# AdaLN and mixture-of-experts kernel: conditioning weights selected by predicated copies, one of two transposed halves copied by VectorE

## The reference, cut to what matters

```python
def _L0_cond_ref(x, subjects, weights, bias):
    w = weights[subjects]              # (128, 32, 32), one of 8 tables for each batch
    b = bias[subjects]
    out = jnp.einsum('bct,bcd->bdt', x, w)
    return out + b[:, :, None]

def _L0_ffn_ref(x, gate_w, w1, w2, w3, sw1, sw2, sw3):
    ...
    scores = jax.nn.softmax((xt @ gate_w.T).astype(jnp.float32), axis=-1)   # 8 experts, top 2
    ...
    z = jax.nn.silu(xt @ sw1.T) * (xt @ sw3.T) @ sw2.T                      # shared, 352 wide
    return (y + z).reshape(B, S, D)

x = x + _L0_ffn_ref(_L0_cond_ref(x, itok_B_0_7, L0_cond_weights, fside_8xS_0), ...)
x = x + _L1_ffn_ref(_L1_cond_ref(x, ...), ...)     # low-rank adapters, then an fp8 gated network
```

## Time and profile before

| | |
|---|---|
| median of 3 runs | 429.93 us (429.85 to 430.27) |
| the profiled execution's own time | 429.1 us |
| its span | 427.3 us |
| TensorE busy | 412.4 us, 97% |
| VectorE busy | 309.2 us, 72% |
| ScalarE busy | 249.0 us, 58% |
| GpSimd busy | 193.2 us, 45% |
| granted TensorE clock | full in all 40 slices |

### The profile page before, as it was taken

One profiled execution on the slowest core, in us unless ns is written; L12 is line 12 of the kernel. 1 busy time (PEld: TensorE's weight loads), 2 busy tenths in 40 slices (PEclk: granted clock), 3 DMA queues, 4 the chain that ended last, 5 costly groups with the idle time before them and its releaser, 6 DMA issues.

```text
span 427.3 us, 8683 instructions
## 1 busy us (share of the span) xinstructions
PE 412.4 (97%) x2954; PEld 331.7 (78%) x2954; DVE 309.2 (72%) x728; ACT 249.0 (58%) x552; POOL 193.2 (45%) x198
## 2 busy tenths in 40 slices
PE   7999789999999999999999999999999999999996
PEld 5567578887889999999999998885665756657553
DVE  5987898997987666666666663759587786777845
ACT  2987544667335665556655654438475494664854
POOL 2404229900544544455445403646575575754020
PEclk9999999999999999999999999999999999999999
DMA  8998300000145554655555622321143232322111
GB/s 250 381 388 297 99 0 2 1 2 0 54 128 179 167 161 144 181 160 158 165 159 176 152 87 74 88 74 51 52 134 95 66 111 74 113 87 61 49 51 50
DMA packets 37290, 50.44 MB, mean 118 GB/s; under 512 B 4504, under 2 KB 30496, under 8 KB 37248
## 3 DMA queue, kind: packets, MB, share of 16 engines
q1 hardware_dynamic: 29600, 31.53, 21.8%
q0 software_dynamic: 6512, 17.71, 15.7%
q10 hardware_dynamic: 1136, 0.65, 0.6%
HBM read 32.18 MB, written 17.69 MB: 117 GB/s over the span
## 4 chain that ended last, share of the span: by engine, by line
PE 81%; ACT 8%; DVE 7%; issue 2%; DMA 2%; POOL 0%; DVEq 0%; ACTq 0%; POOLq 0%
PE bank L1132 16%; PE bank L1134 16%; PE bank L1133 15%; PE bank L1408 13%; PE bank L1423 6%; PE bank L1294 4%; ACT xtr L468 2%; PE bank L1333 2%; PE bank L1332 2%; PE bank L1314 2%; PE bank L1374 2%; ACT xtT L482 2%; PE bank L1222 1%; DVE hsf L761 1%; DMA pick<-in_pick 1%
## 5 line engine op out<-in xcount | busy, mean ns | idle before, releaser
L403 POOL DMA_INDIRECT xg<-kept,perm x71 | 68.1, 959 | 91.2 <-PE bank L1294 54.9
L1408 PE MATMUL bank<-h,wg 128*128 128x512 fp8e4 x256 | 61.6, 380 | 0.2 <-ACT ff L642 0.2
L1132 PE MATMUL bank<-w13h,xgl 128*128 x142 | 48.9, 344 | 0.4 <-issue 0.4
L1408 PEld LDWEIGHTS bank<-h,wg 128*128 128x128 fp8e4 x256 | 22.2, 98 | 33.9 <-ACT ff L642 13.3
L410 POOL DMA_INDIRECT ga<-slots_out,slot x32 | 32.8, 1026 | 33.3 <-SPq L349 17.3
L963 DVE TENSOR_TENSOR hrl<-bank,hrh 128x256 fp32r<-128x256 f32 (+1 forms) x36 | 15.1, 421 | 44.2 <-issue 36.5
L1134 PE MATMUL bank<-w13h,xgh 128*128 x142 | 45.5, 320 | 0.0
L1133 PE MATMUL bank<-w13l,xgh 128*128 x142 | 45.5, 320 | 0.0
L640 ACT ACTIVATE gel<-bank 128x512 bf16<-128x512 f32 x64 | 40.2, 627 | 6.4 <-PE bank L1408 3.2
L410 POOL DMA_INDIRECT gb<-slots_out,slot x32 | 37.7, 1178 | 9.8 <-issue 9.8
L642 ACT ACTIVATE ff<-bank 128x512 bf16<-128x512 f32 x64 | 40.6, 635 | 0.0
(11 more groups left out here) (199 smaller groups left out, 1167.8 us busy)
## 6 DMA issues: line engine op xcount, KB each, us to landing
slots_out<-yr SPq DMA_DIRECT2D x35, 256.0 KB
xres<-in_x SPq DMA_DIRECT2D x7, 512.0 KB, 10.3
kept<-xtr SPq DMA_DIRECT2D x7, 512.0 KB, 7.4
out_x<-fin SPq DMA_DIRECT2D x7, 512.0 KB
w13raw<-in_rw SPq DMA_DIRECT2D x8, 352.0 KB, 4.3
w2raw<-in_rw SPq DMA_DIRECT2D x8, 256.0 KB, 5.6
wgst<-in_wgate SPq DMA_DIRECT2D x16, 128.0 KB
xg<-kept,perm POOLq DMA_INDIRECT x71
```

The costliest lines, as they stand in the source:

```text
L403: pool.indirect_dma_start(out=xg[:, i % 2, j, :], out_offset=None, in_=kept, in_offset=bass.IndirectOffsetOnAxis(perm[:, 2 * i + j:2 * i + ...
L1132: pe.matmul(dst, al, bh, start=first, stop=False, skip_group_check=True)
L1408: ins = pe.matmul(bank[bk][:, :], wg8[:, kk, half, c * P:(c + 1) * P], h8[:, k, kk, :], start=(kk == 0), stop=(kk == KC - 1))
```

## The change

Four edits, and what follows from them. (1) The table is laid out with the choice ahead of the output channel. `wrow` is cleared once, and `select_rows` makes eight predicated copies for each group, one for each choice: where the mask of choice e is set, the table's row of choice e is copied to `wrow`. Each waits for the one before. `prod` is gone. (2) The masks `hot` lie in PSUM, bank 5, columns 0 to 255. Bank 5 being taken, the bias matmul and both halves' raw logits go to bank 4 (columns 0 to 31; 0 to 127 and 128 to 255), and the transposed logits to bank 5, columns 0 to 127, and bank 4, columns 256 to 383; `router(4)` waits until the first half's raw logits are out. (3) ScalarE's `keep_xT` copies only the first half, and VectorE gets a `keep_xT` for the second, with a semaphore `xtT_half`; whoever waited for `xtT_ready` waits for both. (4) VectorE's queue: selections 0 to 3; for i = 4 to 7 `keep_xT(i-4)`, then selection i; then `keep_xT(4)` to `keep_xT(7)`; then `shared_weight_lo(0)` and all the rest as before.

```diff
-        tabr = at("tabr", [P, CH, E], F32, early)
-        hot = at("hot", [P, TILES, E], F32, early)
+        tabr = at("tabr", [P, E, CH], F32, early)
         wrow = at("wrow", [P, TILES, CH], F32, early)
-        prod = at("prod", [P, GT, CH, E], F32, early)
...
+        hot = bank[5][:, 0:TILES * E].rearrange("p (t e) -> p t e", e=E)
+        logit_psum = [bank[5][:, 0:P], bank[4][:, 2 * P:3 * P]]
...
-            pool.wait_ge(s("xtT_ready"), 2)
+            pool.wait_ge(s("xtT_ready"), 1)
+            pool.wait_ge(s("xtT_half"), 1)
...
             def keep_xT(i):
-                for c in range(KC):
-                    act.wait_ge(s("T_done"), i * KC + c + 1)
-                    act.activation(xT_of(i)[:, c, :], bank[6 + c][:, :], ACT.Copy).then_inc(s("xtT_ready"), 1)
+                act.wait_ge(s("T_done"), i * KC + 1)
+                act.activation(xT_of(i)[:, 0, :], bank[6][:, :], ACT.Copy).then_inc(s("xtT_ready"), 1)

             def keep_raw(h):
                 act.wait_ge(s("raw_done"), h + 1)
-                act.activation(lraw[:, h, :], bank[4 + h][:, 0:P], ACT.Copy).then_inc(s("raw_kept"), 1)
+                act.activation(lraw[:, h, :], bank[4][:, h * P:(h + 1) * P], ACT.Copy).then_inc(s("raw_kept"), 1)
...
+            dve.memset(wrow[:, :, :], 0.0).then_inc(s("hot_ready"), 1)
             dve.wait_ge(s("front_in"), 16)
...
             def select_rows(t0, t1):
-
-                link(dve.tensor_tensor(prod[:, 0:t1 - t0], *picks(t0, t1), ALU.mult))
-                dve.tensor_reduce(wrow[:, t0:t1, :].rearrange("p t j -> p (t j)"),
-                                  prod[:, 0:t1 - t0].rearrange("p t j e -> p (t j) e"), AX.X, ALU.add
-                                  ).then_inc(s("rows_ready"), 1)
+                shape = [P, t1 - t0, CH]
+                for e in range(E):
+                    ins = dve.copy_predicated(wrow[:, t0:t1, :], hot[:, t0:t1, e:e + 1].bitcast(I32).broadcast_to(shape),
+                                              tabr[:, e:e + 1, :].broadcast_to(shape))
+                    if e < E - 1:
+                        link(ins)
+                ins.then_inc(s("rows_ready"), 1)
                 selected[0] += 1
                 dve.wait_ge(s("rows_ready"), selected[0])
...
-            for i in range(1, GROUPS):
+            def keep_xT(i):
+                dve.wait_ge(s("T_done"), i * KC + 2)
+                dve.tensor_copy(xT_of(i)[:, 1, :], bank[7][:, :]).then_inc(s("xtT_half"), 1)
+
+            for i in range(1, 4):
                 select_rows(i * GT, (i + 1) * GT)
+            for i in range(4, GROUPS):
+                keep_xT(i - 4)
+                select_rows(i * GT, (i + 1) * GT)
+            for i in range(4, GROUPS):
+                keep_xT(i)
             shared_weight_lo(0)
...
             def transpose_xt(i):
                 if i >= 1:
-                    pe.wait_ge(s("xtT_ready"), i * 2)
+                    pe.wait_ge(s("xtT_ready"), i)
+                    pe.wait_ge(s("xtT_half"), i)
...
             def router(i):
                 h, m = i // HALF, i % HALF
-                pe.wait_ge(s("xtT_ready"), i * 2 + 2)
+                pe.wait_ge(s("xtT_ready"), i + 1)
+                pe.wait_ge(s("xtT_half"), i + 1)
+                if m == 0 and h:
+                    pe.wait_ge(s("raw_kept"), h)
```

More of the change, by code:

```diff
@@ L264, in adaln_ffn @@
         for name in ("ids_in front_in pick_in table_in const_in shapes_in gate_in sw_in hot_ready rows_ready c_link c_prep out_ready bias_made bias_ready "
-                     "cond_done xt_ready T_done xtT_ready gate_spread raw_done raw_kept logit_psum "
+                     "cond_done xt_ready T_done xtT_ready xtT_half gate_spread raw_done raw_kept logit_psum "
                      "m_sub m_exp r_ob r_rank r_digits r_lanes r_places r_listed r_perm r_expert sw_hi sw_split "
@@ L297, in _ @@
         def _(sp):
-            sp.dma_start(tabr[:, :, :].rearrange("p j e -> p (j e)"), table).then_inc(s("table_in"), 16)
+            sp.dma_start(tabr[:, :, :].rearrange("p e j -> p (e j)"), table).then_inc(s("table_in"), 16)
             sp.dma_start(xres[:, 0:2, :], x_t[0][:, 0:2, :]).then_inc(x_first[0], 16)
@@ L471, in shared_x_hi @@
             def shared_x_hi(i):
-                act.wait_ge(s("xtT_ready"), i * 2 + 2)
+                act.wait_ge(s("xtT_ready"), i + 1)
+                act.wait_ge(s("xtT_half"), i + 1)
                 act.wait_ge(s("xs_hi"), i)
@@ L479, in keep_xT @@
             def keep_xT(i):
-                for c in range(KC):
-                    act.wait_ge(s("T_done"), i * KC + c + 1)
-                    act.activation(xT_of(i)[:, c, :], bank[6 + c][:, :], ACT.Copy).then_inc(s("xtT_ready"), 1)
+                act.wait_ge(s("T_done"), i * KC + 1)
+                act.activation(xT_of(i)[:, 0, :], bank[6][:, :], ACT.Copy).then_inc(s("xtT_ready"), 1)
             def keep_raw(h):
                 act.wait_ge(s("raw_done"), h + 1)
-                act.activation(lraw[:, h, :], bank[4 + h][:, 0:P], ACT.Copy).then_inc(s("raw_kept"), 1)
+                act.activation(lraw[:, h, :], bank[4][:, h * P:(h + 1) * P], ACT.Copy).then_inc(s("raw_kept"), 1)
             act.wait_ge(s("bias_made"), 1)
-            act.activation(bias[:, :], bank[5][:, 0:TILES], ACT.Copy).then_inc(s("bias_ready"), 1)
+            act.activation(bias[:, :], bank[4][:, 0:TILES], ACT.Copy).then_inc(s("bias_ready"), 1)
             conditioned(0)
@@ L689, in link @@
                 dve.wait_ge(s("c_link"), links[0])
+            dve.memset(wrow[:, :, :], 0.0).then_inc(s("hot_ready"), 1)
             dve.wait_ge(s("front_in"), 16)
-            dve.tensor_tensor(hot[:, :, :], front[:, 0:TILES].unsqueeze(2).broadcast_to([P, TILES, E]),
+            dve.tensor_tensor(hot, front[:, 0:TILES].unsqueeze(2).broadcast_to([P, TILES, E]),
                               front[:, TILES:].bitcast(F32).unsqueeze(1).broadcast_to([P, TILES, E]), ALU.is_equal
@@ L720, in _ @@
             dve.wait_ge(s("table_in"), 16)
-            dve.wait_ge(s("hot_ready"), 1)
+            dve.wait_ge(s("hot_ready"), 2)
             select_rows(0, GT)
@@ L788, in logit @@
             def logit(h):
-                return bank[4 + h][:, P:2 * P].rearrange("p (j m e) -> p m j e", j=GT, m=HALF)
+                return logit_psum[h].rearrange("p (j m e) -> p m j e", j=GT, m=HALF)
             def half(v, h):
@@ L1161, in router @@
                 h, m = i // HALF, i % HALF
-                pe.wait_ge(s("xtT_ready"), i * 2 + 2)
+                pe.wait_ge(s("xtT_ready"), i + 1)
+                pe.wait_ge(s("xtT_half"), i + 1)
+                if m == 0 and h:
+                    pe.wait_ge(s("raw_kept"), h)
                 for c in range(KC):
                     for j in range(GT):
-                        ins = pe.matmul(bank[4 + h][j * COLS:(j + 1) * COLS, 0:P], gate4[:, c, m, :],
+                        ins = pe.matmul(bank[4][j * COLS:(j + 1) * COLS, h * P:(h + 1) * P], gate4[:, c, m, :],
                                         xT_of(i)[:, c, j * P:(j + 1) * P], start=(m == 0 and c == 0),
@@ L1172, in logits @@
                 pe.wait_ge(s("raw_kept"), h + 1)
-                pe.transpose(bank[4 + h][:, P:2 * P], lraw[:, h, :], ident).then_inc(s("logit_psum"), 1)
+                pe.transpose(logit_psum[h], lraw[:, h, :], ident).then_inc(s("logit_psum"), 1)
             pe.wait_ge(s("c_prep"), 1)
@@ L1183, in _ @@
             for j in range(GT):
-                ins = pe.matmul(bank[5][j * CH:(j + 1) * CH, 0:TILES], pick[:, BATCH:BATCH + CH].bitcast(F32),
+                ins = pe.matmul(bank[4][j * CH:(j + 1) * CH, 0:TILES], pick[:, BATCH:BATCH + CH].bitcast(F32),
                                 hot_out[:, j * TILES:(j + 1) * TILES], start=True, stop=True, tile_position=(0, j * CH))
@@ L1541 @@
         "consts": _constants(),
-        "table": np.tile(L0_cond_weights.transpose(1, 2, 0).reshape(CH, CH * E), (BPT, 1)),
+        "table": np.tile(L0_cond_weights.transpose(1, 0, 2).reshape(CH, E * CH), (BPT, 1)),
         "x": x.reshape(TOK, D),
```

## The result

The changed kernel takes 439.12 us (median of 5 runs, 437.32 to 440.50) against 429.85 (429.12 to 430.27): ratio 1.022, interval 1.0189 to 1.0251. It is slower by 9.3 us. The prediction was 437.7, with 432.6 to 442.0. The profiled execution took 437.32, the quickest of the five; its span is 435.5 us, 8.2 over the span before.

A forecast was written before the change was run, and what follows sets the result against it. TensorE, busy 97%, was taken as the bound, with ScalarE setting the early loop's 2.43 us beat. The first shared matmul moving from 30.87 to 38.7 adds 7.8 us to 429.93, giving 437.7; range 432.6 to 442.

The forecast's parts named there:

- VectorE's order costs, and the shift goes to the end whole: VectorE's queue moves the first shared matmul from 30.87 to 38.7; the 7.8 us reach the end, give or take 1.
- Selection 2.56 a group: On VectorE, eight linked predicated copies 0.32 us apart take 2.56 us a group, against 2.54 before.
- a 512 copy: VectorE's copy of one 128x512 transposed half from PSUM, taken at 0.70 us with the gap.
- Rounds of 3.26, then 2.2 and 2.0: TensorE's rounds: 3.26 us at VectorE's pace from group 1, then 2.2 to transposes 6 and 2.0 to transposes 7.
- Tail 2.83 plus 0.25 for a stretch beside GpSimd: Three residue steps behind VectorE's copy 7, no longer hidden, 2.83 us; 0.25 more for one stretched multiply expected to return.
- The clearing of `wrow` costs nothing: On VectorE at the start: at most 1.22 us, ahead of the numbers' arrival at 3.08, so nothing.
- The two cheap-copy and dear-copy rivals: Predicated copies at two elements a cycle, 433.2 us, chance 0.15; or at two cycles an element, 446, chance 0.07.
- The clock rival: TensorE's clock falls after idling about 3 us before the first shared matmul: +1.7 us, 439.4, chance 0.12.
- up to 1 us from how later VectorE and GpSimd work overlaps: Behind the first shared matmul: give or take 1 us on the 7.8 us shift.

The follow-up runs named there:

- c: Changed kernel with the three residue steps put between VectorE's copies 4, 5, 6 and 7; 434.99 us, ratio 1.0123.
- b: Changed kernel with the multiply and reduction back, table and masks as before, VectorE still copying one half of every group; 437.81 us, ratio 1.0196.
- a: Changed kernel with both halves copied by ScalarE again, VectorE still selecting by predicated copies; 430.92 us, ratio 1.0028.
- d: Changed kernel with idle matmuls on ones where TensorE waits, ahead of transposes 1, 3, 4, 5 and the first shared matmul; 437.98 us.
- j: Changed kernel with 40 idle matmuls on ones ahead of the first shared matmul only; 437.92 us.
- l: Changed kernel with multiply and reduction back, VectorE's half copies kept, 40 idle matmuls ahead of the first shared matmul; 437.00 us.
- f: Changed kernel with predicated copies batched over groups, ScalarE copying both halves of groups 0 to 2, residue steps between VectorE's last copies; 430.75 us.

## Why the prediction was right, point by point

- **VectorE's order costs, and the shift goes to the end whole.** Right in the mechanism: first shared matmul 39.18, forecast 38.7; rest of the span 396.3, in a profile without a late dip, against 396.4 before. Run c shows the bare tail (3.06 us in the profile), b and a split the shift into 7.1 and 1.1.
- **Selection 2.56 a group.** Measured 2.70; a linked copy starts 0.337 after the last, not 0.32. Over eight groups +1.1, of which half was given back: a 512 copy frees the queue after 0.61, not 0.70 (0.36 over four), and the first selection began at 5.23 instead of 5.48. The latter is luck of this profile: the start moves with the pick transfer, 5.15 to 5.68 over the profiles of the changed kernel. So the last selection ended 0.5 late. From the first selection to the first shared matmul the forecast had 33.2 us, and 33.95 were measured.
- **Rounds of 3.26, then 2.2 and 2.0.** Measured 3.32, then 2.23 and 2.15, so that the last transposes started 0.8 late (34.48 instead of 33.7).
- **Tail 2.83 plus 0.25 for a stretch beside GpSimd.** The tail was 2.82; the stretch did not return, the predicated copies beside GpSimd's casts (16.63 to 19.3) took 2.68 like the others. That the tail's sum was too high made up for part of the rounds that were too short: 38.7 came nearer to 39.18 than its terms did.
- **The clearing of `wrow` costs nothing.** 0.91 us, over at 1.92, ahead of 3.14.
- **The two cheap-copy and dear-copy rivals** fell with the 304 ns. By the figure of the Trainium skill, page VectorE: DVE Perf Modes, section on the TRN2 errata, for a source in PSUM (120 + elements cycles), a copy would be 258 ns, an estimate. The trace does not agree, and its next row of the kind (292, L796) was nearer.
- **The clock rival was held too cheaply.** It had 0.12, as something that happens to the kernel or not. The runs show it as something that happens to executions: in the place I named, ahead of the first shared matmul, in some runs and not in others, at 1.4 to 2.5 us each (I had 1.7), so the median holds about half of it. The row that I held against it, an almost empty stretch of 1.5 us at a clock of 1.00, is no evidence: by the durations TensorE worked at the low rate on both sides of it (313 ns for a matmul on ones).
- **Where the 1.4 us between 437.7 and 439.12 went.** Half is the queue's own: the way to the first shared matmul was 0.7 us longer than forecast, by the pitch and the rounds above. The other half is the term that was put at nothing: "7.8 us go to the end whole" needed 0.7 to 1.0 us on top (9.27, 9.36 and 9.59 in the three measurements of the changed kernel, less 8.56) for the wait that the change creates on TensorE. Runs d and j, with that wait filled, have none of it.
- **The other place was missed.** TensorE also stands empty for 2.7 us ahead of transposes 1. It costs nothing at the end, or 0.2 us, because VectorE is later still.
- **Unsettled:** a, c and l have 0.4 to 0.9 us more behind the first shared matmul than the changed kernel without a late dip. I expected up to 1 us from how later VectorE and GpSimd work overlaps, and did not trace it.

## What to carry to other kernels

Before moving work to an engine, read its own slack in that stage: here 2.2 us stood against 5.5 us of copies, and what queued behind them (three residue steps) became bare although nobody touched it. Where the receiving engine sits idle between the moved pieces, put the queued work there; the same instructions in another order gave back 3.7 to 4.0 us. And a wait that a change creates on TensorE can cost more than its length: here 0.7 to 1.0 us of the median on top of 3 us, and 24 or 40 matmuls on ones in the gap took that back.

## What the runs showed of the hardware that was not expected

- A predicated copy from SBUF under a mask in PSUM takes 304, 447 and 600 ns for 128, 256 and 384 fp32 elements, 1.1 to 1.2 ns per further element.
- TensorE's granted clock dropped to its lower level, 1.2 GHz, behind an empty 2.7 us in all three profiles of the changed kernel, but behind an empty 3.0 us at 36 to 39 us in only one of them. With multiply and reduction it stayed up behind an empty 2.21 us in b and dropped behind 2.56 in l.
- In the first 10 us of the profiles of the kernel before, the changed kernel and f the recorded clock reads 1.00 while the matmuls run at about half rate (312 to 314 ns for one on ones against 220 later), in f up to 18.0 us (up to 475 ns for a transpose against 273). The durations tell more than the record.
